# A graph layer's adjacency counts built from items of 128 edges for two destinations instead of 256 slots for five

## What is computed

```python
def _gcn_conv(x, W, b, src, dst, n):
    h = x @ W
    # self-loops appended to src and dst, deg = edges per destination
    norm = dinv[src_sl] * dinv[dst_sl]
    out = jax.ops.segment_sum(h[src_sl] * norm[:, None], dst_sl, num_segments=n)
    return out + b

x = x + relu(gcn_conv(relu(gcn_conv(layernorm(x), W1, b1)), W2, b2))
x = x + ffn_top2_of_8_experts(layernorm(x))
```

## Time and profile before

| | |
|---|---|
| time of the profiled execution | 2288.68 us |
| its span | 2287.0 us |
| median of three runs | 2290.35 us |
| mean granted TensorE clock | 0.975 |
| TensorE matmul busy | 2104.1 us (92%) |
| TensorE weight load busy | 1416.2 us (62%) |
| VectorE busy | 1577.0 us (69%) |
| ScalarE busy | 819.5 us (36%) |
| GpSimd busy | 474.3 us (21%) |

### The profile page before, as it was taken

The page is one execution under the profiler, slowest core; times in us unless marked ns, Lnnn a source line. Parts: engine busy times, 40 slices in busy tenths (PEclk is TensorE's granted clock), DMA queues, the critical chain, the costliest instruction groups (busy, mean ns, idle before and its releaser), DMA issues. The chain is left out here.

```text
span 2287.0 us, 43796 instructions
## 1 busy us (share of the span) xinstructions
PE 2104.1 (92%) x14031; PEld 1416.2 (62%) x14032; DVE 1577.0 (69%) x5153; ACT 819.5 (36%) x1862; POOL 474.3 (21%) x628
## 2 busy tenths in 40 slices
PE   1599999999999999679999999998299999999997
PEld 1256666666666666335555555554189999999996
DVE  7899999999999999223444434344766666666664
ACT  4544444444444444201111212112054444444442
POOL 3600000000000000000000000000055655565653
PEclk9999999999999999889999999999599999999998
DMA  6022222222222222154655566673423332332322
GB/s 192 30 85 85 85 114 85 85 113 86 85 103 96 86 94 105 59 203 168 211 185 189 207 227 225 209 244 111 173 53 48 50 50 47 49 49 47 52 48 27
DMA packets 73895, 255.02 MB, mean 112 GB/s; under 512 B 10407, under 2 KB 50792, under 8 KB 59528
## 3 DMA queue, kind: packets, MB, share of 16 engines
q1 hardware_dynamic: 31160, 181.37, 21.0%
q0 software_dynamic: 28464, 58.79, 12.0%
q10 hardware_dynamic: 14112, 12.85, 1.6%
HBM read 137.89 MB, written 115.08 MB: 111 GB/s over the span
## 5 line engine op out<-in xcount | busy, mean ns | idle before, releaser
L677 PE MATMUL mp_o<-rows,m_counts 128*128 128x512 f16 x2401 | 597.8, 380 | 2.9 <-ACT m_counts L783 1.7
L1526 PE MATMUL rp_o<-rows,r_adj 128*128 128x512 f16 x2401 | 551.1, 380 | 33.5 <-DMA r_adj<-adj 33.5
L597 DVE TENSOR_SCALAR m_oh_cell<-m_cells,m_edge_cell 128x246 f16<-128x246 f16 x2500 | 521.8, 284 | 0.0
L775 ACT ACTIVATE m_counts<-mp 128x490 f16<-128x490 f32 x586 | 339.3, 583 | 461.7 <-PE mp L712 461.6
L1526 PEld LDWEIGHTS rp_o<-rows,r_adj 128*128 128x128 f16 x2401 | 235.5, 99 | 282.1 <-issue 36.6
L712 PE MATMUL mp<-m_oh_cell,m_oh_lane 128*128 128x245 f16 x2500 | 366.1, 272 | 27.5 <-DVE m_oh_cell L597 17.9
L677 PEld LDWEIGHTS mp_o<-rows,m_counts 128*128 128x128 f16 x2401 | 233.0, 97 | 188.5 <-issue 7.3
L712 PEld LDWEIGHTS mp<-m_oh_cell,m_oh_lane 128*128 128x128 f16 x2500 | 245.5, 99 | 163.4 <-DVE m_oh_cell L597 17.1
L2018 PE MATMUL fp_h<-f_xt,w 128*128 128x256 f16 x2688 | 304.5, 274 | 0.2 <-DVE f_xt L2114 0.2
L2037 PE MATMUL fp_y<-w,f_hh 128*128 x2688 | 302.4, 273 | 0.0
L2018 PEld LDWEIGHTS fp_h<-f_xt,w 128*128 x2688 | 263.9, 98 | 31.2 <-issue 0.6
(11 more groups left out here) (213 smaller groups left out, 1633.5 us busy)
## 6 DMA issues: line engine op xcount, KB each, us to landing
adj<-m_counts SPq DMA_DIRECT2D x49, 1568.0 KB, 5.2
r_adj<-adj SPq DMA_DIRECT2D x49, 1568.0 KB, 6.7
r_raw<-in_L_ffn_W_dram POOLq DMA_DIRECT2D x16, 1024.0 KB
w_parts<-r_parts POOLq DMA_DIRECT2D x8, 1024.0 KB, 5.7
w<-w_parts SPq DMA_DIRECT2D x4, 2048.0 KB
rows<-in_x_dram SPq DMA_DIRECT2D x7, 896.0 KB, 11.2
r_x<-in_x_dram SPq DMA_DIRECT2D x49, 128.0 KB, 2.0
out_dram<-r_x ACTq DMA_DIRECT2D x49, 128.0 KB, 1.7
```

The source lines that it names most:

```text
L597: oh = nc.vector.tensor_scalar(oh_cell[:, slot(n) + i, :], cells[:], edge_cell[:, item:item + 1], None, ALU.is_equal)
L677: mm = nc.tensor.matmul(ps_o[q], counts[:, q, s, :], k.rows[0][:, s, :], start=i == 0, stop=i == BLOCKS - 1)
L775: last = nc.scalar.activation(counts[:, q, :, lo - b * P:hi - b * P].rearrange("p h (a d) -> p h a d", d=STEP), halves, ACT.Copy, scale=CO ...
L1526: mm = nc.tensor.matmul(ps_o[q], adj[:, q, s * P:(s + 1) * P], rows[:, s, :], start=s == 0, stop=s == BLOCKS - 1)
```

## The change

Two destinations share one item of 128 slots. A bank still takes ten destinations, as five items of 98 columns (49 blocks x 2), each written by one matmul. There are 3125 items. The cell values are kept in bf16, each twice, as the lanes are, and VectorE compares the cells of three banks (15 items, 1470 elements) in one `tensor_tensor`; the lanes of three banks are now 1920 elements. TensorE waits once per three banks for both. The tables have 5 columns of 128 banks with 5 items each: 5 searches in `heads` (three on VectorE, two on ScalarE), 5 gathers of 512 entries of `dst`, 25 searches in these (15 on VectorE, 10 on ScalarE), 25 gathers of 132 edges. One limit is left for the degrees. `DEG_AT`, `ROWS_END` and `FIRST_AT` are each one bank later.

```diff
-STEP = 5
-ITEMS5 = 2
-CAP = ITEMS5 * P
-SPAN = 2 * STEP
-BANK_ITEMS = 2 * ITEMS5
+STEP = 2
+BANK_ITEMS = 5
+SPAN = BANK_ITEMS * STEP
...
+COL_ITEMS = BANK_ITEMS * P
+CELLS2 = STEP * BLOCKS
+CHUNK = 4 * P
+FOLDS = ((0, 2), (2, 4), (4, 5))
-SEEK_V = 5
+SEEK_V = 3
+FINE_V = 3
-DEG_AT = 6
-ROWS_END = 23
+DEG_AT = 7
+ROWS_END = 24
-FIRST_AT, FIRST_PARTS = 14, 6
+FIRST_AT, FIRST_PARTS = 15, 6
...
             for c in range(COLS):
-                pool.wait_ge(first_ready, 1 if c < SEEK_V else 2)
-                start = bass.IndirectOffsetOnAxis(ap=first_i[:, c:c + 1], axis=0)
-                pool.indirect_dma_start(out=edges[:, c, :], out_offset=None, in_=k.io["edges"], in_offset=start).then_inc(got[c], 16)
+                pool.wait_ge(first_ready, c + 1)
+                for j in range(BANK_ITEMS):
+                    start = bass.IndirectOffsetOnAxis(ap=first_i[:, c, j:j + 1], axis=0)
+                    pool.indirect_dma_start(out=edges[:, c, j, :], out_offset=None, in_=k.io["edges"], in_offset=start).then_inc(got[c], 16)
...
+            for c in range(COLS):
+                dve.wait_ge(chunk_in[c], 16)
+                for j in range(FINE_V):
+                    seek = nc.vector.tensor_scalar(junk_v[:, j * CHUNK:(j + 1) * CHUNK], low(chunk[:, c, :]), aim[:, c, j:j + 1],
+                                                   start_f[:, c:c + 1], ALU.is_lt, ALU.add, accum_out=first[:, c, j:j + 1])
+                dve.wait_ge(fine, (BANK_ITEMS - FINE_V) * (c + 1))
+                link(nc.vector.tensor_scalar(first[:, c, FINE_V:], over[:, c, :], -0.5, middle_f[:, c:c + 1], ALU.mult, ALU.add))
+                nc.vector.tensor_copy(first_i[:, c, :], first[:, c, :]).then_inc(first_ready, 1)
+                if c < 2:
+                    loads(c)
...
+            for c in range(COLS):
+                dve.wait_ge(got[c], 16 * BANK_ITEMS)
+                shape = [P, BANK_ITEMS, P]
+                nc.vector.tensor_tensor(code[:, c], rows_d[:, c, :, 0:P], bc(aim[:, c, :, None], shape), ALU.subtract)
+                if c:
+                    dve.wait_ge(codes_ready, c)
+                link(nc.vector.tensor_single_scalar(edges_h, rows_s[:, c], 7, ALU.arith_shift_right))
+                nc.vector.scalar_tensor_tensor(lanes[:, c], edges_h, -float(P), rows_s[:, c], ALU.mult, ALU.add).then_inc(lanes_ready, 1)
+                nc.vector.scalar_tensor_tensor(code[:, c], code[:, c], float(BLOCKS), edges_h, ALU.mult, ALU.add).then_inc(codes_ready, 1)
+                loads(c + 2)
+                if c:
+                    compare(c - 1)
...
-                        for i in range(BANK_ITEMS):
-                            item = n * BANK_ITEMS + i
-                            oh = nc.vector.tensor_scalar(oh_cell[:, slot(n) + i, :], cells[:], edge_cell[:, item:item + 1],
-                                                         None, ALU.is_equal)
-                        oh.then_inc(cell_ready, 1)
+                            for width, out, row, table, ready in ((P, oh_lane, k.lane_b, edge_lane, lane_ready),
+                                                                  (CELLS2, oh_cell, cells, edge_cell, cell_ready)):
+                                pairs = [P, items, width // 2, 2]
+                                nc.vector.tensor_tensor(
+                                    out[:, r:r + items].rearrange("p r (v t) -> p r v t", t=2),
+                                    bc(row[:].rearrange("p (v t) -> p v t", t=2)[:, None, :, :], pairs),
+                                    bc(table[:, at, :][:, :, None, :], pairs), ALU.is_equal).then_inc(ready, 1)
...
-                            mm = nc.tensor.matmul(bank(n)[:, half_bank:half_bank + CELLS5], oh_lane[:, slot(n) + i, :],
-                                                  oh_cell[:, slot(n) + i, 0:CELLS5], start=i % ITEMS5 == 0,
-                                                  stop=i % ITEMS5 == ITEMS5 - 1)
+                            mm = nc.tensor.matmul(bank(n)[:, i * CELLS2:(i + 1) * CELLS2], oh_lane[:, slot(n) + i, :],
+                                                  oh_cell[:, slot(n) + i, :], start=True, stop=True)
...
+                items = bank(n)[:, 0:BANK_ITEMS * CELLS2].rearrange("p (a h d) -> p h a d", a=BANK_ITEMS, d=STEP)
...
+                    last = nc.scalar.activation(
+                        counts[:, q, :, lo - b * P:hi - b * P].rearrange("p h (a d) -> p h a d", d=STEP),
+                        items[:, :, (lo - first_dst) // STEP:(hi - first_dst) // STEP, :], ACT.Copy, scale=COUNT_SCALE)
```

More of the change, by code:

```diff
@@ L350, in build_layer_one @@
         block = st.enter_context(nc.Block())
[L352 removed]
+        ps_n = ps[:, 0:COLS * SPAN]
         def bank(n):
@@ L378, in _ @@
             sp.wait_ge(deg_ready, 1)
-            with nc.allow_non_contiguous_dma(reason="five numbers per window"):
-                sp.dma_start(deg_d.rearrange("(c p) j -> p c j", p=P), deg[:]).then_inc(deg_out, 16)
+            with nc.allow_non_contiguous_dma(reason="ten numbers per window"):
+                sp.dma_start(deg_d.rearrange("(c p) j -> p c j", p=P), deg[:].rearrange("p c j t -> p c (j t)")).then_inc(deg_out, 16)
             sp.wait_ge(deg_out, 16)
@@ L490, in _ @@
             link(nc.vector.tensor_copy(cells[:], cells_i[:]))
-            loads(0)
-            for part, done in ((range(0, SEEK_V), chunks_a), (range(SEEK_V, COLS), chunks_b)):
-                dve.wait_ge(done, 16 * len(part))
-                for c in part:
-                    seek = nc.vector.tensor_scalar(junk_v[:, c * P:(c + 1) * P], low(chunk[:, c, :]), aim[:, c:c + 1], start_f[:, c:c + 1],
-                                                   ALU.is_lt, ALU.add, accum_out=first[:, c:c + 1])
-                link(seek)
-                cs = slice(part[0], part[-1] + 1)
-                nc.vector.tensor_copy(first_i[:, cs], first[:, cs]).then_inc(first_ready, 1)
-                loads(1 if part[0] == 0 else 2)
@@ new lines, in count_below @@
+            def count_below(c):
+                pe.wait_ge(signed_ready, c + 1)
+                pe.wait_ge(below_ready, c + 1)
+                for t, src in enumerate((signed, below)):
+                    per = src[:, c * COL_ITEMS:(c + 1) * COL_ITEMS].rearrange("p (w j) -> p w j", j=BANK_ITEMS)
+                    for j in range(BANK_ITEMS):
+                        at = c * SPAN + j * STEP + t
+                        mm = nc.tensor.matmul(ps_n[:, at:at + 1], per[:, :, j], one_h[:], start=True, stop=True)
@@ new lines, in _ @@
+            act.wait_ge(signs, COLS - SEEK_V)
+            for c in range(COLS):
+                act.wait_ge(chunk_in[c], 16)
+                for j in range(FINE_V, BANK_ITEMS):
+                    o = (j - FINE_V) * CHUNK
+                    if c:
+                        act.wait_ge(fine, (BANK_ITEMS - FINE_V) * (c - 1) + j - FINE_V + 1)
+                    nc.scalar.activation(junk_a[:, o:o + CHUNK], chunk[:, c, :], ACT.Sign, bias=aim_neg[:, c, j:j + 1],
+                                         accum_out=over[:, c, j - FINE_V:j - FINE_V + 1]).then_inc(fine, 1)
```

248 lines of the change are left out of this document (95 added, 153 removed).

## The result

The changed kernel takes 2183.41 us, the median of four runs (2181.15 to 2183.73), against 2290.40 us for the kernel before beside it: a ratio of 0.953, 95% interval 0.9518 to 0.9542. Forecast were 2181 us and a range of 2154 to 2226. The profiled execution took 2183.68 us; its span is 2182.0, 105.0 less than before.

A forecast was written before the change was run, and what follows sets the result against it. TensorE was taken to set the bank loop's pace, with VectorE 9% behind, and VectorE that of the first 125 us. Terms: -123 + 20 + 7.4 - 13 - 1.3 = -110 us, giving about 2181 us, range 2154 to 2226.

The forecast's parts named there:

- Bank matmuls: TensorE in the bank loop: five 98-column matmuls take 0.225 us a bank against 0.43, 123 us less over some 600 banks.
- Ends of blocks: At block ends TensorE waits for ScalarE's copy or emptying, mean 0.41 us; 49 ends give 20 us back.
- VectorE in the loop: Bank loop: cell comparison 0.92 us per three banks; VectorE needs 11.0 us a block against TensorE's 15, so hidden.
- rival 2: Cell comparison runs at one element per cycle, its collisions with the block's own work show: 2211 us; chance 0.12.
- First banks: Stretch after the tables up to block 0's sum: 13 us shorter, with GpSimd's and ScalarE's work hidden; bounds 5 and 20.
- Tables: Table building before the bank loop, up to the degrees: costs 7.4 us more, ending at 75.1 us; bounds 2 and 13.
- The main term: Bank loop together: 123 us less from its matmuls, 20 us given back at block ends, one bank (1.3 us) already counted.

The follow-up runs named there:

- runs 1 and 2: Changed kernel with each 98-column bank matmul issued as two of 49 columns: 2208.20 us; with bank matmuls cut to their first 49 columns (incomplete result): 2140.98 us.
- Runs 6 to 8: Changed kernel, product a bank later: 2195.63 us; with normalizations split, sum in 12 parts: 2160.41, or transposes a bank earlier: 2183.55; kernel before with 12 parts: 2282.75.
- Run 3: Changed kernel with the cells of three banks compared by 15 `tensor_scalar` operations of 98 elements instead of one `tensor_tensor`: 2274.39 us, ratio 0.9932 to the kernel before.
- Run 5: Changed kernel with ScalarE taking every third of GpSimd's 49 row normalizations: 2178.24 us, ratio 0.9506 to the kernel before.
- the kernels with the stall: Ten matmuls (and its repeat), half columns, 15 comparisons, 12 parts, earlier transposes: ScalarE's table copies stood still, and GpSimd's normalizations started at 75.2 to 76.1 us.

## Why the prediction was right

**Bank matmuls: right.** 45 ns a matmul and 0.203 us a bank, predicted 0.205; runs 1 and 2 show that it is columns. The Trainium skill's figure for short pairs ("TensorE: Matmul & The Clock Gate", section "Back-to-back issue gap", about 81 ns at 128 columns) is not borne out here: 98 columns with a load each go at 45 ns. No run has 128 columns in the bank; from 45 ns and the 19 ns between 49 and 98 columns I would estimate 57. The rows of one-column pairs were the better witness.

**Ends of blocks: right in kind and size.** Predicted was that three of five products wait 0.4 us and the other ends collide with the emptying, 0.41 us a block. The loads wait 0.41 us for the copy 28 times in 46 blocks and stop 18 times, 9.1 us in all, before the sum's first part, 20.5 us together for the forecast 20. A block (the mean of 46, from one block's transposes to the next's) fell from 17.28 to 15.08 us, 2.20, where its 12.755 banks of 0.203 would be 2.59: it gives back 0.39. Runs 6 to 8 show that this is the order of work: with 12 parts those waits of the matmul row are down to 0.9 us.

**VectorE in the loop: right.** 0.92 us for the cells, 69% busy for a forecast of 75; rival 2 (1.7 us for the cells) falls. Run 3 shows how near it is: with 15 small operations VectorE is the bound.

**First banks: the step that failed.** The text had it that GpSimd's 49 rows "end at 111 at the latest" and are hidden. They ended at 120.06, and the stretch gave 4.9 us instead of 13. I had added the 36.7 us that they took beside the old mix of VectorE's work. That figure was no property of GpSimd: it is 32.3, 36.7, 51.2 or 56.6 us as VectorE runs less or more work with two inputs from SBUF beside it (`tensor_tensor` and the low halves). The change itself, by joining the cells into `tensor_tensor`, slowed GpSimd. Run 5 shows that its lateness cost some 6 of the 8 us. The other 2 are about what the last nine matmuls of block 0's sum lose at the lower clock (4.02 us for 2.12), a term that the forecast didn't have; with the rows split they still take 3.75.

The Trainium skill says it in "SBUF — State Buffer", section "Who interferes with whom": a VectorE instruction with two SBUF inputs contends with a GpSimd instruction that reads SBUF. The trace agrees (3.07 us a row beside `tensor_tensor` without a gap, 0.55 for the shortest); by that rule the cover I counted on had to be checked.

**Tables: mis-sized.** Predicted +7.4, measured +1.5. The first chunk came at 18.5 us, not 21; a fine search took 0.80 us with a pitch of 0.73, close to the forecast; the counting comparison 0.47, not 0.7; the columns 5.75 us each, not 6.1. In the kernels with the stall the term is 8 to 9 us, by something I had not foreseen.

**How much of the hit is luck.** The tables came 6 us better than forecast and the first banks 8 us worse, and that these two nearly cancel is luck. Either alone would have left the time inside the range. The main term, 104 us in the bank loop for the 103.4 measured, owes nothing to it.

## What to carry to other kernels

Cost short matmuls by their columns and look for the shortest pair in the trace to see the floor. When a stretch of the bound engine shrinks, list what the next engine must finish inside it, here a copy with 0.04 us of play, and see whether other work can be spread in between: here a constant from 10 to 12 was worth more than either shift of a stage that was tried. Do not carry a GpSimd duration over when VectorE's instructions beside it change their kind. And when an effect comes and goes between kernels, see whether it goes with the kernel or with the group of runs before calling it either.

## What the hardware showed that was not expected

- A load of 128 columns and a matmul of 49 follow each other every 26 ns, as did pairs of one column, though the profile gives the load alone 99 ns.
- GpSimd's same 49 instructions took 32.3 to 56.6 us, by what VectorE ran beside them; changing only the form of VectorE's cell comparison took them from 36.7 to 56.6 in one kernel and from 51.2 to 32.3 in the other.
- Reading PSUM in runs of two columns for runs of five cost ScalarE nothing: 0.58 us for 490 columns both times.
- Nine matmuls of 512 columns took 4.02 us at a granted clock of 0.50, after TensorE had been idle for 4.3 us, and 2.12 at 1.00.
- In the tables ScalarE's copies stood still twice, for some 6 and 6.7 us, in six executions of eleven with the same table code; whether that goes with the kernel or with the chip is open.

The fastest kernel with the whole result is the changed one with the normalizations split and the sum in 12 parts: 2160.41 us, 0.943 of the kernel before.
